# Expert tiles of a mixture-of-experts stage filled across twelve routings instead of four, and addressed through a list

## The reference

```
xn = LN(x)
agg[n] = sum over edges with dst = n of edge_weight * xn[src]        # 106250 edges, sorted by dst
x2 = x + agg @ gnn_weight + linear_attention(xn) + bout              # K^T V of 8 heads, over all rows
y  = LN(x2)
logits = y @ gate_w + gate_b                                         # 16 experts
the two best experts of each row, weights p = softmax of the two logits
h  = relu(y @ w1[e] + b1[e])           # 256 -> 512
r  = h @ w2[e] + b2[e]                 # 512 -> 256
out = x2 + LN(y + p0 * r(e0) + p1 * r(e1)) * gamma + beta
```

## Time and profile before

| what | value |
|---|---|
| time, median of 3 runs | 1648.58 us (1646.62 to 1650.65) |
| the profiled execution | 1632.83 us, its span 1631.1 us |
| busy: PE, DVE, ACT, POOL | 70%, 36%, 28%, 61% of the span |
| mean granted TensorE clock | 0.872 of full speed |
| DMA traffic | 332.12 MB, 204 GB/s over the span |
| gathers of the edges, first and last start | 53.1 and 1355.4 us |

### The profile page before, as it was taken

One profiled execution on the slowest core, in us unless ns is written; L12 is line 12 of the kernel. 1 busy time (PEld: TensorE's weight loads), 2 busy tenths in 40 slices (PEclk: granted clock), 3 DMA queues, 4 the chain that ended last, 5 costly groups with the idle time before them and its releaser, 6 DMA issues. The chain is left out here.

```text
span 1631.1 us, 24092 instructions
## 1 busy us (share of the span) xinstructions
PE 1137.6 (70%) x7296; PEld 879.2 (54%) x7296; DVE 594.4 (36%) x1789; ACT 452.8 (28%) x1238; POOL 1003.1 (61%) x1090
## 2 busy tenths in 40 slices
PE   0299998987660398898850698998422899856881
PEld 0155555545540287787630587786321788746770
DVE  6455554444451122322341123332340232353544
ACT  4144333322220133333220233333110333322330
POOL 3577777777527767776657776756757772337303
PEclk9999999998775699999965799999665999888995
DMA  9496333333213656789634767987435688749993
GB/s 336 147 319 202 104 107 104 105 105 98 75 40 123 202 179 231 263 272 341 213 92 145 252 185 258 324 304 276 122 103 176 207 302 281 243 144 329 381 359 96
DMA packets 157786, 332.12 MB, mean 204 GB/s; under 512 B 26097, under 2 KB 98289, under 8 KB 157521
## 3 DMA queue, kind: packets, MB, share of 16 engines
q1 hardware_dynamic: 73264, 162.47, 28.4%
q0 software_dynamic: 49296, 134.68, 26.6%
q10 hardware_dynamic: 35088, 33.30, 6.0%
HBM read 271.36 MB, written 58.98 MB: 203 GB/s over the span
## 5 line engine op out<-in xcount | busy, mean ns | idle before, releaser
L684 POOL DMA_INDIRECT ring<-normed_rows,src_sb x831 | 797.1, 959 | 348.3 <-issue 285.7
L1309 PE MATMUL ps<-room 128*128 128x128 f32 x2208 | 290.2, 288 | 27.6 <-DMA room<-in_w1b 18.4
L1309 PEld LDWEIGHTS ps<-room 128*128 128x128 f32 x2208 | 276.7, 204 | 34.1 <-ACT room L777 17.5
L1185 PE MATMUL ps<-ring,S 128*32 128x256 f32 x1680 | 124.4, 437 | 222.6 <-DMA ring<-normed_rows,src_sb 192.7
L1322 PE MATMUL ps<-room 128*128 128x256 f32 x1104 | 266.0, 384 | 8.8 <-issue 6.2
L1120 DVE TENSOR_TENSOR desk<-ps,room 128x256 f32<-128x256 f32 x158 | 66.9, 424 | 554.1 <-PE ps L1322 531.6
L1322 PEld LDWEIGHTS ps<-room 128*128 128x128 f32 x1104 | 202.5, 194 | 32.3 <-issue 8.2
L796 ACT ACTIVATE room<-ps,room 128x128 f32<-128x128 f32 x552 | 157.3, 368 | 186.4 <-PE ps L1309 186.1
L1185 PEld LDWEIGHTS ps<-ring,S 128*32 128x32 f32 x1680 | 54.3, 122 | 264.4 <-issue 235.8
L1212 PE MATMUL ps<-room,tT 128*128 128x512 f32 x392 | 179.3, 601 | 0.1
L662 POOL DMA_INDIRECT rows_by_slot<-X,slot_i x98 | 96.7, 987 | 119.3 <-DVEq L1110 90.7
(11 more groups left out here) (151 smaller groups left out, 1157.2 us busy)
## 6 DMA issues: line engine op xcount, KB each, us to landing
room<-in_w2b SPq DMA_DIRECT2D x100, 640.0 KB
room<-in_w1b SPq DMA_DIRECT2D x100, 514.0 KB, 5.4
room<-rows_by_slot SPq DMA_DIRECT2D x158, 128.0 KB
results_by_slot<-desk ACTq DMA_DIRECT2D x158, 128.0 KB
ring<-normed_rows,src_sb POOLq DMA_INDIRECT x831
normed_rows<-X SPq DMA_DIRECT2D x7, 896.0 KB, 7.9
rows_by_slot<-desk ACTq DMA_DIRECT2D x1, 6272.0 KB, 25.3
rows_by_slot<-desk ACTq DMA_DIRECT2D x1, 5760.0 KB, 26.0
```

The source lines that it names most:

```text
L684: pool.indirect_dma_start(out=ring[:, b % 2 * BT + m, :], out_offset=None, in_=table, in_offset=bass.IndirectOffsetOnAxis(ap=src_sb[:, b * ...
L1185: mm = pe.matmul(acc[b % 2][w * W:(w + 1) * W, :], S[b % 2][:, m, :], ring[:, b % 2 * BT + m, :], start=(t == 0), stop=(t == GT - 1), skip ...
L1309: mm = pe.matmul(hps[:, f * TS:(f + 1) * TS], w1_sb[g % WB][:, k * F + f * P:k * F + (f + 1) * P], xgT[s][:, k, :], start=(k == 0), stop=( ...
```

## The change

There are now two parts, `PT = (0, 36, 49)`, and twelve routings, which end after row tile 6, 12, 16, 20, 24, 28, 32, 36, 40, 44, 47 and 49 (`SUB`). Each routing ranks only its own two to six row tiles, and fills up the tiles that the routings before it left open: per expert it keeps how much room is left in the open tile and where it is. A tile goes onto a list when it is full, or at the end of a part. So the tiles are no longer in order of experts but in the order in which they get full, and a new stage, `list`, turns the list into three tables (expert, tile number, whether to load weights) by two small matmuls on PE and five steps on DVE. SP and ACT read the tile number into a register before they load a tile's rows and store its results.

How many listed tiles each routing works off ("visits") is fixed when the kernel is built: 4, 12, 8, 8, 8, 8, 8 and 31 in the first part, 0, 8, 6 and 28 in the second, 129 together. For the given input 118 of these hold a tile. Of the 11 others 3 only skip their products, and 8 lie in runs that one branch leaves out as a whole (`left_out`). By the rule of three buffers 116 visits load weights. Both tables get their own memory, and more of it is zeroed: 11.9 and 5.9 MB of rows, 2.5 and 2.5 MB of results, where it was 6.3, 5.8 and 0.3 MB.

The scatters are cut into twelve pieces of 4 to 12 transfers. All results of a part must be stored before its rows are picked up, and the first part now has 36 row tiles.

Shortened diff (the arithmetic of `slots` is longer than shown):

```diff
-PT = (0, 16, 30, 42, NT)
-NPART = len(PT) - 1
-MOST = max(b - a for a, b in zip(PT, PT[1:]))
+PT = (0, 36, NT)
+SUB = (0, 6, 12, 16, 20, 24, 28, 32, 36, 40, 44, 47, NT)
+NPART, NSUB = len(PT) - 1, len(SUB) - 1
+MOST = max(b - a for a, b in zip(SUB, SUB[1:]))
+SUB_PART = [max(p for p in range(NPART) if PT[p] <= a) for a in SUB[:-1]]
+PART = [max(p for p in range(NPART) if PT[p] <= q) for q in range(NT)]
 ROWS_OF = [min(N, PT[p + 1] * P) - PT[p] * P for p in range(NPART)]
-NPOS = [(2 * n + E * (TS - 1)) // TS for n in ROWS_OF]
-SURE = [-(-2 * n // TS) for n in ROWS_OF]
-POS0 = [sum(NPOS[:p]) for p in range(NPART + 1)]
-NPOSITIONS = POS0[NPART]
-PART = [max(p for p in range(NPART) if PT[p] <= q) for q in range(NT)]
-XROWS = [max(NPOS[i::2]) * TS + 2 * P for i in range(2)]
-DUMMY = NPOS[-1] * TS
+NTILES = [(2 * n + E * (TS - 1)) // TS for n in ROWS_OF]
+XROWS = [(n + 4) * TS for n in NTILES]
+MOSTLY, FIRST_RUN, RUN = 8, 2, 4
+def ends_part(s):
+    return SUB[s + 1] in PT
+def runs():
+    out, at = [], 0
+    for p in range(NPART):
+        seen, floors = 0, []
+        for s in range(NSUB):
+            if SUB_PART[s] != p:
+                continue
+            rows = min(N, SUB[s + 1] * P) - PT[p] * P
+            mostly = max(0, 2 * rows // TS - MOSTLY)
+            if not ends_part(s):
+                n = max(0, mostly - seen)
+                if n:
+                    out.append((s, at, n, False))
+                floors.append((max(0, -(-(2 * rows - E * (TS - 1)) // TS)), seen))
+            else:
+                n = NTILES[p] - min([seen] + [sure + seen - before for sure, before in floors])
+                first = mostly + 2 * MOSTLY - seen - FIRST_RUN
+                out.append((s, at, first, False))
+                for i in range(first, n, RUN):
+                    out.append((s, at + i, min(RUN, n - i), True))
+            seen += n
+            at += n
+    return out, at
+RUNS, VISITS = runs()
+VISITS_OF = [sum(n for s, _, n, _ in RUNS if s == t) for t in range(NSUB)]
+LISTS = [sum(n > 0 for n in VISITS_OF[:s + 1]) for s in range(NSUB)]
+FIRST_OF = [sum(VISITS_OF[:s]) for s in range(NSUB + 1)]
+PART_END = [sum(n for s, _, n, _ in RUNS if SUB_PART[s] <= p) for p in range(NPART)]
 WB = 3
...
-            what, p, _ = routes.pop(0)
-            work.append((what, p))
+            what, s, _ = routes.pop(0)
+            work.append((what, s))
             if what == "slots":
-                at = min(b + 2 - (not tiles), NB)
-                ready[p] = at + 1
-                pool[at].append(("scatter", p))
-                tiles.extend((p, j) for j in range(NPOS[p]))
+                sent[s] = min(b + 2 - (not tiles), NB)
+                pool[sent[s]].append(("scatter", s))
+            if what == "list":
+                ready[s] = sent[s] + 1
+                tiles.extend((r, j) for r, run in enumerate(RUNS) if run[0] == s for j in range(run[2]))
             return 0.5
...
-            if GROUPS[g][1] in PT:
-                p = PART[GROUPS[g][0]]
-                routes.extend([("rank", p, now + 4.0), ("slots", p, now + 8.0)])
+            if GROUPS[g][1] in SUB:
+                s = SUB.index(GROUPS[g][1]) - 1
+                routes.extend([("rank", s, now + 4.0), ("slots", s, now + 8.0)])
+                if VISITS_OF[s]:
+                    routes.append(("list", s, now + 14.0))
...
+        def skip(eng, done, g0, n, each=1):
+
+            if n:
+                after(eng, done, each * g0)
+                eng.sem_inc(done, each * n)
+
+        def run(eng, stages, slot):
+
 
             for stage in SLOTS[slot]:
-                if stage[0] in stages:
-                    stages[stage[0]](*stage[1:])
+                if stage[0] != "moe" or not RUNS[stage[1]][3]:
+                    if stage[0] in stages:
+                        stages[stage[0]](*stage[1:])
+                elif stage[2] == 0:
+                    s, g0, n, _ = RUNS[stage[1]]
+                    eng.wait_ge(listed, LISTS[s])
+                    expert = eng.value_load(etab[0:1, g0:g0 + 1], min_val=0, max_val=E)
+                    with eng.If(expert < E):
+                        for j in range(n):
+                            stages["moe"](stage[1], j)
+                    with eng.Else():
+                        stages["left_out"](stage[1])
...
-            def load_rows(p, j):
-                if j < NPOS[p]:
-                    g = POS0[p] + j
+            def load_rows(r, j):
+                s, g0, n, _ = RUNS[r]
+                if j < n:
+                    g, p = g0 + j, SUB_PART[s]
+                    t = sp.value_load(ttab[0:1, g:g + 1], min_val=0, max_val=NTILES[p] + 1)
                     after(sp, xg_turned, g - XB + 1)
-                    sp.dma_start(xg[g % XB], xs[p % 2][j * TS:(j + 1) * TS, :]).then_inc(xg_in[g % XB], 16)
+                    sp.dma_start(xg[g % XB], xs_tiles[p][bass.ds(t, 1)].rearrange("a p d -> (a p) d")).then_inc(xg_in[g % XB], 16)
...
+                new = sp.value_load(fresh[0:1, g:g + 1], min_val=0, max_val=1)
+                with sp.If(new > 0):
...
+            def moe(r, j):
+                s = RUNS[r][0]
                 if j == 0:
-                    sp.wait_ge(slots_done, p + 1)
-                    load_weights(p, 0)
-                    sp.wait_ge(scattered, 32 * PT[p + 1])
...
+                    sp.wait_ge(listed, LISTS[s])
+                    load_weights(r, 0)
+                    sp.wait_ge(scattered[s], 32 * (SUB[s + 1] - SUB[s]))
...
-            def scatter(p):
-                pool.wait_ge(slots_done, p + 1)
-                pool.wait_ge(y_normed, GATE_AT[PT[p + 1] - 1] + 1)
-                if p == 0:
-                    pool.wait_ge(zero_out, 16 * 3)
-                if p >= 2:
-                    for s in range(XB):
-                        pool.wait_ge(xg_in[s], 16 * rows_loaded(s, p - 2))
-                for q in range(PT[p], PT[p + 1]):
+            def scatter(s):
+                p = SUB_PART[s]
+                pool.wait_ge(slots_done, s + 1)
+                pool.wait_ge(y_normed, GATE_AT[SUB[s + 1] - 1] + 1)
+                if s == 0:
+                    pool.wait_ge(zero_out, 16 * 2 * NPART)
+                for q in range(SUB[s], SUB[s + 1]):
                     for k in range(2):
                         pool.indirect_dma_start(
-                            out=xs[p % 2], out_offset=bass.IndirectOffsetOnAxis(ap=slot_i[:, k, q:q + 1], axis=0),
-                            in_=X2[:, q, :], in_offset=None).then_inc(scattered, 16)
+                            out=xs[p], out_offset=bass.IndirectOffsetOnAxis(ap=slot_i[:, k, q:q + 1], axis=0),
+                            in_=X2[:, q, :], in_offset=None).then_inc(scattered[s], 16)
 
             def pick(f):
-                    pool.wait_ge(ys_out[s], 16 * positions_with(s, p))
+                    pool.wait_ge(ys_out[s], 16 * visits_with(s, PART_END[p]))
...
-                if q in (2, 6):
+                if q % 4 == 2 and q // 4 < NPART:
                     zero_rows(xs[q // 4][:, :], XROWS[q // 4])
-                if q == 10:
-                    zero_rows(ys[NPART - 1][DUMMY:, :], 2 * P)
+                if q % 4 == 0 and q // 4 < NPART:
+                    surely = -(-2 * ROWS_OF[q // 4] // TS) * TS
+                    zero_rows(ys[q // 4][surely:, :], XROWS[q // 4] - surely)
...
+            def slots(s):
+                if SUB[s] in PT:
+
+                    for t in (room_left, next_row, given, lined, seen, line_e, line_t):
+                        dve.memset(t[:, :], 0.0)
...
+                dve.tensor_tensor(over[:, :], count[:, :], room_left[:, :], ALU.subtract)
...
+                dve.tensor_tensor(lt3, lt3, each(jump, nt), ALU.mult)
+                dve.tensor_tensor(is_below[:, :], is_below[:, :], jump[:, :], ALU.mult)
...
                 dve.drain().then_inc(slots_done, 1)
...
+                if VISITS_OF[s]:
+                    dve.tensor_scalar(sel[:, 0:VISITS_OF[s]], iota[:, 0:VISITS_OF[s]], line_from[:, :], None, ALU.is_equal)
+                    dve.scalar_tensor_tensor(out=seen[:, :], in0=seen[:, :], scalar=float(VISITS_OF[s]), in1=lined[:, :],
+                                             op0=ALU.add, op1=ALU.min)
+                dve.drain()
+                dve.tensor_tensor(line_e[:, :], line_e[:, :], kept[:, :], ALU.add)
+                dve.tensor_reduce(line_no[:, :], value[:, :], AX.X, ALU.add)
+                dve.drain()
+                dve.tensor_tensor(line_t[:, :], line_t[:, :], line_no[:, :], ALU.add)
+                dve.drain().then_inc(lined_up, 1)
...
+            def list_visits(s):
...
+                dve.wait_ge(turned, TURN_AT["list", s] + 1)
+                row = experts[:, WB + g0:WB + g0 + n]
+                dve.tensor_scalar(row, listps[0][:, 0:n], float(E), None, ALU.add)
+                dve.drain()
+                dve.tensor_scalar(empty[:, 0:n], row, float(E), None, ALU.is_ge)
```

(16 more changed lines are left out.)

407 lines of the change are left out of this document (246 added, 161 removed).

## The result

The changed kernel takes 1723.04 us (1716.39 to 1729.73, 4 runs), the kernel before 1647.6 (1645.45 to 1650.65, 4 runs): ratio 1.0457, 95% interval 1.0412 to 1.0501. That is 75 us slower; forecast were 11 us faster, and the range ended at 1668. The profiled execution has a span of 1728.0 us, 108 more than the 1620 at which the prediction's walk along POOL's stream ended. Of these 108, 22 are the choice of the executions: the profiled one before lay 15.8 us under the median of its runs, the profiled one here lies 6.7 over it. By the medians 1723 stands against 1637, 86 us.

A forecast was written before the change was run, and what follows sets the result against it. POOL's stream was taken to bound up to the last gather at 1362 us, then a tail to 1620, -11 us against the profiled 1631.1; with the runs' median 15.75 higher, the forecast was 1637, range 1604 to 1668.

The forecast's parts named there:

- walk along POOL's stream: Following POOL's transfers and waits batch by batch, with PE's slots at their earlier cost, to an end at 1620 us.
- What bounds the kernel: POOL's stream bounds up to the last gather: 53 + 1156 work + 148.5 waits + 4 stretched = 1362 us.
- The zeros: Zero fills of 22.8 MB instead of 12.3 cost POOL nothing; up to 15 us if that cover fails.
- What I cost at nothing: Terms taken as 0: more zeros, fewer PE products outside the tail, 16 more weight loads, register reads of tile numbers.
- A routing's chain: In each routing, slots_done comes 24 us after the batch's matmuls, where it took some 26.3 before.
- the first rival: More waits at routings: a chain of 30 us and longer slots 22 to 27, +36, 1673 us; chance 0.22.
- PE between the routings: POOL's waits on PE up to the last gather, 59 us in all.
- nothing waits for that part: In slots 41, 46, 52, 63, 68 DVE's work behind slots_done delays nothing, POOL being 15 us or more ahead.
- The early pick: Ahead of the first part's pick, POOL waits 14.7 us for that part's last result.
- Then 22 tiles ... 4.7 us: 1464 + 21 x 4.7: In the tail, 22 full tiles instead of 25, at 4.7 us each, from 1464 to 1563.
- First full tile ... 8.7: The tail's first full tile comes 8.7 us after the last part's four scatters, at 1464.
- The descriptors: Rival: DVE's added operations lock GpSimd out of writing descriptors, +20 us and the gain gone, 1657; chance 0.05.

The follow-up runs named there:

- f1: The changed kernel with its four zero fills at rows 2, 10, 14 and 18 of the keys and values instead of 0, 2, 4 and 6: 1702.6 us.
- e2: The changed kernel with the first group of finished rows picked in the tail, not early: 2202.2 us, 1.033 of the kernel before, on a slower kind of chip.
- g4: The changed kernel with later zero fills, stores three groups behind, a last-part first run of 22 visits, and the planner's branched-visit price 3.9 instead of 0.5: 1685.5 us.
- e5: The changed kernel with the last part's unbranched run of 22 visits instead of 17, the six left in runs of 4 and 2: 1705.8 us.
- e6: The changed kernel with later zero fills, SP's stores three groups behind, and the last part's first run of 22 visits: 1675.2 us, 1.019 of the kernel before.
- f2: The changed kernel with twelve more drained 128x16 steps in each routing, ahead of slots_done: 1760.4 us, 1.070 of the kernel before.

## Why the prediction was wrong, step by step

The forecast was 11 us faster and the kernel came out 75 slower. The steps that failed are, in us: a fill of zeros that cost 22.7 and not 0, tiles in the tail that took 24.6 more because of branched starts, PE's stands at the routings (16.5, 12.4 and part of the 11.2), and 11.6 ahead of the tail's first tile.

**What bounds the kernel** was right: 53 + 1156 + 211.0 = 1420, and the last gather ended at 1425.7. The gathers' count and price held; only the waits were wrong, by 62.5 us of 63.7.

**The zeros** ("What I cost at nothing") failed: up to 15 us if the cover fails, taken as 0, and measured 22.7. I asked whether full queues delay a gather. The profile of before could not show what happened: there the fill ahead, of 6.3 MB at 88.9, landed after 25.3 us, and the next one's issue, at 109.1, took 0.52 us. I did not ask what an engine does that issues behind much that is still under way on its own queue. f1 shows the step.

**A routing's chain** was right: 24 us, measured 23.1 in slot 41 and 22.8 to 23.5 in slots 36, 46, 52 and 63. So the first rival, which is on the right side, names the wrong cause; its price of 1673 came from a chain of 30. The scatters waited 11.2 us more than in the walk, chiefly because PE reached the batch late: 5.5 us behind its last gather in slot 41 (869.6 and 864.1) and 6.0 in slot 46, not 2, and 12.0 in slot 36.

**PE between the routings**: 16.5 us mis-sized. The step that failed is "nothing waits for that part", said of the end of `slots` and the list: PE waited for it, 10.8 us in slot 41 with the next batch's rows already gathered, and 107.0 in ten places. Of POOL's long waits on PE three were somewhat over the walk (14.5, 10.2 and 9.8 for 9.2, 8.6 and 8.5), those up to batch 29 were 7 us under it together, and nine short ones of 0.4 to 4.2 us after batch 30, 16 us together, I had at 0.8. In 1000 to 1200 it was granted 0.76, before 0.87 (busy us of each engine, granted clock, DMA share, GB/s), the changed kernel first:

```profile
1000.00:1200.00 200.00, 120.74 (x828) 97.90 (x829) 54.19 (x250) 42.49 (x123) 140.41 (x147) 0.76 0.66 223
```

```profile
1000.00:1200.00 200.00, 155.20 (x1080) 126.82 (x1079) 64.12 (x217) 55.97 (x169) 132.15 (x137) 0.87 0.70 236
```

828 products take 120.7 us, 0.146 each, and 1080 took 155.2, 0.144 each. By this mean the slower clock would cost some 2 us here, an estimate that leaves out that the products are not the same mix; what the rows do show is that PE stands more, and does less work in the same time.

**The early pick**, 14.7 taken and 27.1 measured, is slot 61, which took 46.0 us (1276.43 to 1322.47). e2 and g4 speak against the pick and against the place of the visits as the cause: without either, POOL waited as long for PE (37.3 for 38.0 us in e2, and 182.8 for 185.6 in all in g4).

**"Then 22 tiles ... 4.7 us: 1464 + 21 x 4.7"** failed for a reason that was in the code of the change: two of the tail's runs begin behind a branch (the gaps of 11.0 and 19.2 us between full tiles), and rows and weights are asked for only within a run. e5 gives 4.80 a tile without such starts, where the walk had 4.7. I had counted the branches as a gain ("17 of the 22 visits now are not" behind one).

**"First full tile ... 8.7"** was 20.7 behind the last of the four scatters (1520.5 to 1541.2): SP stood in the store of finished rows up to 1530.7, waiting for DVE, while the list had been ready at 1523.3. e6 gave 7 us back. Picks and finished rows at the very end: 50.0, not 44; nothing was tried there.

**The descriptors**: DVE is busy 78 us longer between 50 and 1728 (635.9 us, before 557.6) and POOL's gathers have a mean of 0.958 us (0.959 before) and a median of 0.946, as before. The rule of the Trainium skill ("SBUF — State Buffer", section "SBUF: two separate sides"), by which such operations lock GpSimd out, would have stretched them; in this kernel no run shows it.

What stays open: by the medians e5 gains 10 us less and f2 loses 18 us more than by the traces. Much of it is which execution was profiled, as these lie 6 to 11 us from their medians; what makes the executions differ isn't shown. Open are also the last 6 us of the tail, and through what a routing costs its 10 us.
